# Routed experts of a four-layer transformer kernel: the gating multiply as a step of its own, the second selection and the first half's statistics one tile later

## The chip, the cores and the metric

The kernel runs on one core of one Trainium2 chip. The metric is the device time of one execution in microseconds (us), the median of several runs. The core has TensorE (PE, matrix products; its weight loads are listed as PEld), VectorE (DVE, elementwise work), ScalarE (ACT), GpSimd (POOL) and SyncE (SP, which here only issues DMAs). Each engine works through its own list of instructions in order, and waits on semaphores that other engines raise.

## The reference, cut to what matters

Four layers follow one another on 1024 tokens of 512 numbers. Each is a cross attention and a feed-forward part, each with a layer norm in front and its result added to x. The change is in the feed-forward part of the second layer, a low-rank mixture of 64 experts of rank 8, of which each token uses 16:

```python
q = einsum('bsd,rd->bsr', x, Wq_w);  scores = einsum('bsr,er->bse', q, keys)
top_vals, top_idx = top_k(scores, 16)
gate = sum(one_hot(top_idx, 64) * softmax(top_vals)[..., None], axis=-2)
z = einsum('bsd,nd->bsn', x, A_w).reshape(..., 64, 8)
z_gated = (z * gate[..., None]).reshape(..., 512)
out = einsum('bsn,on->bso', z_gated, B_w) * 2.0
x = x + out
```

Here x on the right of the first lines is the layer norm of x. What comes next, in the third layer's attention, is again a layer norm of x.

The last feed-forward part of the network (fourth layer) has weights that are to be quantised to 16 levels per block of 64 and back ("nf4") before they are used. This has nothing to do with the experts, but it is computed beside them.

## The kernel before, in words

**Tiles.** The 1024 tokens are 8 tiles of 128 (`TILES`); a half is 4 tiles (`TPH`). Everything is fp32, and a product of two fp32 matrices is done as three passes over high and low parts (helper `product`, L1739: 12 matmuls for a contraction over 512).

**The order of the work.** `schedule` writes out one list of steps for the whole program. Each engine walks the same list and, for each step, issues the instructions that its own handler of that name has. A step that stands earlier in the list stands earlier on every engine that takes part in it.

**The steps of the experts.** Per half: `route1` copies the router's scores out of PSUM and picks each token's 16 largest with two rounds of eight maxima (DVE, L1415 to L1426), ACT takes the exponentials, and `gates1` turns them into gates (DVE, L1432 to L1435). Per tile t: `z1` is the product of the normalised x with A (PE, 12 matmuls `bank<-slots,xT`); `zt1` begins on DVE with the gating multiply, `zg<-bank,gates` (L1446), which PE then transposes (4 small matmuls `bank<-ident,zg`, L1939); ACT copies the transposed tile out as the high part (`zT<-bank`, L946) and DVE takes the low part (`zT<-bank,zT`, L1201). `b1` is the product with B (PE, 12 matmuls `bank<-slots,zT`), which DVE adds to x (L1303) and, for tiles 1 to 3 of a half, follows with the statistics of the tile before (L1318). `stats` for layer index 4 ends the statistics of one half of the tokens: one more BN_STATS, 4 aggregations, a chain of 13 tiny operations with a wait behind each, and 4 normalisations into `xn` (L1224 to L1245).

In the loop over tiles PE's order is: transposes of tile t, `b1` of tile t-1, `z1` of tile t+2. So `z1` runs one tile ahead of its use and `b1` one tile behind.

**The background.** `with_background` spreads the steps of the nf4 work over the list between `q0` of the first layer and `raw_gate2` of the third, in proportion to the table `WEIGHT` of the real steps. Each block of weights takes 15 steps `nf`: DVE compares the weights with a bound (`nf_y<-nf_w`, L1681) and PE adds the result up (`nf_sum`, one matmul, L2109). The buffer `nf_y` has 6 places (`STAIR_RING`), so DVE's step i waits for PE's sum i-6. At a block's end come a wait for all its sums and `nf_w<-bank,nf_a` (L1691); the next block begins with `nf_w<-nf_w,nf_r` (L1675), and SP loads and stores each block.

**The weights.** Each chunk of weights is loaded by SP into `staging`, then split: ACT writes the high part (`slots<-staging`, L961), POOL the low part (L864). The slot of a chunk is reused after its last product; the split of the first of the `k2` weights, step `("split", 59)`, waits for `z1` of tile 7 on ACT. `spread_splits` places the splits in the list.

**Banks.** PE's products take 7 PSUM banks in turn (`claim`), and each claim waits for the last reader of what stood there.

Of the kernel before, what the change touches and what calls it, by code (L numbers as in the profile page):

```python
# [19 lines left out]
TPH = TILES // 2  # L20
# [85 lines left out]
def schedule(only=None):  # L106

    steps = []
# [61 lines left out]

    steps += [("route1", 0), ("turn", 3, 1), ("raw_route1", 1), ("z1", 0), ("gates1", 0)]
    for t in range(TILES):
        if t + 1 < TILES:
            steps.append(("z1", t + 1))
        steps.append(("zt1", t))
        if t >= 1:
            steps.append(("b1", t - 1))
        if t < 2:
            steps.append(("route1", 1) if t == 0 else ("gates1", 1))
        if t - 1 == TPH - 1:  # L180
            steps.append(("stats", 4, 0))
    steps += [("b1", TILES - 1)] + [("k2", c) for c in range(KT)] + [("bias2",), ("c2",), ("turn", 4, 0), ("stats", 4, 1)]
    if only == 4:
# [176 lines left out]
def build(nc, a, out, known, only=None):  # L360
    ctx = ExitStack()
    with ctx:
        sig = Signals(nc, ctx, known)

        def sb(name, shape, dt, scope=ctx):
            return scope.enter_context(nc.sbuf_tensor(name, shape, dt))
# [56 lines left out]
        k2 = sb("k2", [P, 2, KT, B * CTX], F32R, l)  # L423
# [59 lines left out]
        def psum(key):  # L483
            return banks[sig.bank_for(key)]
# [100 lines left out]


        base = schedule(only)
        if only is None or only == 7:
            jobs = []
# [37 lines left out]
        steps = []  # L627
# [45 lines left out]
        else:  # L673
            n_chunks = len(chunks)
            steps = [(kind, i) for i in range(n_chunks) for kind in ("load", "split")] + base
# [15 lines left out]
        def weight(name, part):  # L691

            _, p, dims, _, dest, _ = chunks[chunk_no[name]]
            if dest is not None:
                return dest[part]
            size = int(np.prod(dims))
            return flat(slots[0:p, slot_no[name] % NSLOT, part, 0:size], dims)
# [143 lines left out]
        def split_source(i):  # L841
            _, p, dims, *_ = chunks[i]
            return flat(staging[0:p, i % 2, 0:int(np.prod(dims))], dims)
# [3 lines left out]
        def _(pool):  # L847
# [12 lines left out]
            def split(i):  # L860
                pool.wait_ge(*sig.when("weight_high", i))
                _, p, dims, *_ = chunks[i]
                hi, lo = weight(chunks[i][0], 0), weight(chunks[i][0], 1)
                g.tensor_tensor(lo, split_source(i), hi.bitcast(FP32), ALU.subtract).then_inc(*sig.mark("weight_low", i))  # L864
# [323 lines left out]
        def _(dve):  # L1188
# [9 lines left out]
            def low(stage, key, dst, src, hi):  # L1198

                dve.wait_ge(*sig.when(f"{stage}_high", key))  # L1200
                v.tensor_tensor(dst, src, hi.bitcast(FP32), ALU.subtract).then_inc(*sig.mark(f"{stage}_low", key))  # L1201
# [236 lines left out]
            def z1(t):  # L1438
                pass

            def zt1(t):
                dve.wait_ge(*sig.when("z1_product", t))
                dve.wait_ge(*sig.when("gates1", t // TPH))
                if t >= 2:
                    dve.wait_ge(*sig.when("zt1_product", t - 2))
                v.tensor_tensor(zg[:, t % 2].rearrange("p (e r) -> p e r", e=NE),  # L1446
                                psum(("z1", t))[:].rearrange("p (e r) -> p e r", e=NE),
                                gates[:, t].unsqueeze(2).broadcast_to((P, NE, RANK)), ALU.mult)\
                    .then_inc(*sig.mark("gated1", t))
                low("zt1", t, zT[:, t % 2, 1], psum(("zt1", t))[:].rearrange("p (k n) -> p k n", k=KT), zT[:, t % 2, 0])  # L1450

            def b1(t):
# [231 lines left out]
            def nf_end(n, m, f):  # L1684
# [3 lines left out]
                if m == 2:  # L1688
# [3 lines left out]

            handlers = {"stats": stats, "turn": turn, "k0": k0_, "kc0": kc0_, "q0": q0_, "scores0": scores0,
                        "scale0": scale0, "low3": low3, "pv0": pv0, "o0": o0, "up0": up0, "down0": down0, "scores1": scores1,
                        "probs1": probs1, "gates1": gates1, "pv1": pv1, "router1": router1, "route1": route1, "z1": z1, "zt1": zt1, "b1": b1, "k2": k2_,
                        "m2": m2_, "bias2": bias2, "gate2": gate2, "moe": moe, "hid2": hid2, "out2": out2,
                        "values3": values3, "scores3": scores3, "pv3": pv3, "o3": o3, "up3": up3,
                        "down3": down3, "nf_max": nf_max_, "nf": nf, "nf_end": nf_end}
# [496 lines left out]
```

## Time and profile before

| | |
|---|---|
| median of 3 runs | 1546.58 us (1543.73, 1546.64, 1546.58) |
| profiled execution | 1543.49 us, span in the trace 1541.8 us |
| busy over the span | PE 1374.1 us (89%), DVE 974.8 (63%), ACT 459.4 (30%), POOL 288.6 (19%) |
| chain of waits, by engine | PE 72%, DVE 18%, issue 3%, DMA 2%, ACT 2% |
| the experts' tiles | from the first `zg` at 893.3 us to the last add to x, 972.5 us |

The profile comes from one execution, and times inside it are counted from the start of its span. The chain of waits follows the work that ended last back to its releasers. PE ends the program almost everywhere, so a gap of PE is the first thing to look for in a stage. In the rows below, "[4.67 <-DVE zg L1446]" behind a row says that the engine sat idle for 4.67 us in front of it and that the write of `zg` ended that. Rows of the timeline merge like instructions in a run: the first number is the start, the second the time from the first's start to the last's end.

### The profile page before, as it was taken

What the parts mean: (1) busy time and instruction counts of PE and PEld (TensorE: products, weight loads), DVE (VectorE), ACT (ScalarE), POOL (GpSimd) and SP (SyncE); (2) the same over time, 40 slices, a digit from 0 to 9 for tenths busy, and PEclk for the clock granted to TensorE, in tenths of its full rate; (3) what the DMA queues carried; (4) which work ended last, traced back from release to release, by engine and by line L of the source; (5) the groups of instructions that cost most, each with busy time, mean ns of one, the idle gap of its engine ahead of it and who ended that gap; (6) DMA issues with size and microseconds to landing.
All of it is one profiled execution on the core that took longest, in us unless ns stands there. A gap on an engine that the chain in (4) does not pass through costs nothing.

```text
span 1541.8 us, 18547 instructions
## 1 busy us (share of the span) xinstructions
PE 1374.1 (89%) x6429; PEld 1060.3 (69%) x6429; DVE 974.8 (63%) x2208; ACT 459.4 (30%) x991; POOL 288.6 (19%) x170
## 2 busy tenths in 40 slices
PE   6699799999999998997976687788999899899998
PEld 5467577777777666876854365656888677678886
DVE  3677767868787865554588756875447677455142
ACT  3343324332443432421324100332221453222010
POOL 4110111111111111210212001312452331022120
PEclk9889899999999999999997699999999899799999
DMA  4412423233222321222213001310111100012001
GB/s 150 143 51 61 116 78 108 74 102 92 71 80 62 112 57 57 67 65 69 88 35 76 27 28 47 102 36 2 55 55 44 53 28 1 1 41 68 26 20 55
DMA packets 99389, 96.38 MB, mean 63 GB/s; under 512 B 13122, under 2 KB 72402, under 8 KB 99298
## 3 DMA queue, kind: packets, MB, share of 16 engines
q1 hardware_dynamic: 98786, 94.35, 21.0%
q8 instruction: 54, 0.88, 0.2%
q0 software_dynamic: 512, 0.85, 0.2%
q14 instruction: 37, 0.30, 0.1%
HBM read 84.34 MB, written 10.82 MB: 62 GB/s over the span
## 4 chain that ended last, share of the span: by engine, by line
PE 72%; DVE 18%; issue 3%; DMA 2%; ACT 2%; SPq 2%; POOL 1%; DVEq 0%; ACTq 0%
PE bank L1739 51%; PE bank L2109 6%; PE bank L1833 5%; DVE nf_y L1681 3%; PE bank L1823 2%; PE bank L2044 2%; PE bank L2064 2%; PE bank L1766 1%; DVE xn L1245 1%; DVE st L1318 1%; PE bank L2053 1%; PE bank L1824 1%; DVE xT L1201 1%; DVE rs L1212 1%; DVE st L1224 1%
## 5 line engine op out<-in xcount | busy, mean ns | idle before, releaser
L1739 PE MATMUL bank<-xT,slots 128*128 128x512 f32 (+1 forms) x1920 | 459.0, 396 | 5.0 <-DVE xT L1201 3.2
L864 POOL TENSOR_TENSOR slots<-staging,slots 128x1024 fp32r<-128x1024 f32 (+4 forms) x97 | 229.4, 2367 | 1074.5 <-ACT slots L961 1074.4
L1739 PEld LDWEIGHTS bank<-xT,slots 128*128 128x128 f32 (+1 forms) x1920 | 348.1, 182 | 102.2 <-issue 9.3
L1681 DVE TENSOR_SCALAR nf_y<-nf_w 128x512 fp32r<-128x512 f32 (+2 forms) x495 | 244.8, 523 | 29.7 <-PE bank L2109 28.4
L2109 PE MATMUL bank<-nf_y,nf_d 128*128 128x512 f32 (+2 forms) x495 | 164.2, 416 | 19.7 <-DVE nf_w L1691 11.7
L1739 PE MATMUL bank<-slots,h 128*128 128x512 f32 (+1 forms) x728 | 176.5, 401 | 4.5 <-DVE h L1344 4.5
L1739 PEld LDWEIGHTS bank<-slots,h 128*128 128x128 f32 (+1 forms) x728 | 139.0, 191 | 39.3 <-DVE h L1344 5.4
L961 ACT ACTIVATE slots<-staging 128x1024 fp32r<-128x1024 f32 (+4 forms) x97 | 98.1, 1018 | 189.5 <-PE bank L1739 175.5
L2109 PEld LDWEIGHTS bank<-nf_y,nf_d 128*128 128x128 f32 (+1 forms) x495 | 92.2, 192 | 59.2 <-issue 28.8
L995 ACT ACTIVATE e<-bank,mx 128x320 f32<-128x320 f32 x128 | 66.4, 523 | 211.0 <-DVE mx L1282 207.5
L1833 PE MATMUL bank<-eT,v 128*96 128x256 f32 (+1 forms) x384 | 111.1, 412 | 0.0
L1301 DVE TENSOR_TENSOR x<-bank,x 128x512 f32<-128x512 f32 x56 | 38.7, 691 | 113.3 <-PE bank L1739 113.3
L1766 PE MATMUL bank<-ident,xn 128*128 128x128 f32 x256 | 52.4, 357 | 49.8 <-DVE xn L1245 47.0
L1739 PE MATMUL bank<-slots,q 96*128 96x512 f32 x384 | 95.5, 397 | 1.1 <-DVE q L1201 1.1
L1201 DVE TENSOR_TENSOR q<-bank,q 96x256 fp32r<-96x256 f32 (+1 forms) x96 | 48.7, 508 | 70.1 <-ACT q L946 69.7
L1739 PEld LDWEIGHTS bank<-slots,q 96*128 96x128 f32 x384 | 71.6, 188 | 18.8 <-issue 2.2
L1766 PEld LDWEIGHTS bank<-ident,xn 128*128 128x128 f32 x256 | 40.5, 181 | 61.2 <-issue 50.0
L1833 PEld LDWEIGHTS bank<-eT,v 128*96 128x96 f32 (+1 forms) x384 | 57.6, 170 | 34.7 <-issue 25.0
L1823 PE MATMUL bank<-ident,e 128*128 128x128 f32 x256 | 49.1, 287 | 31.9 <-DVE e L1289 31.7
L1739 PE MATMUL bank<-k,q 96*128 96x320 f32 x384 | 69.6, 317 | 2.8 <-DVE q L1201 2.8
L1739 PEld LDWEIGHTS bank<-k,q 96*128 96x128 f32 x384 | 62.2, 193 | 10.1 <-DVE q L1201 3.9
L1823 PEld LDWEIGHTS bank<-ident,e 128*128 128x128 f32 x256 | 34.7, 148 | 38.9 <-issue 19.9
(251 smaller groups left out, 1678.0 us busy)
## 6 DMA issues: line engine op xcount, KB each, us to landing
staging<-in_L_wqkT SPq DMA_DIRECT2D x16, 480.0 KB, 3.7
nf_out<-nf_w SPq DMA_DIRECT2D x30, 256.0 KB, 2.1
staging<-nf_out SPq DMA_DIRECT2D x30, 256.0 KB, 2.9
staging<-in_L_woT SPq DMA_DIRECT2D x16, 384.0 KB, 3.7
staging<-in_L_w SPq DMA_DIRECT2D x12, 512.0 KB, 3.7
nf_r<-nf_rcp SPq DMA_DIRECT2D x40, 128.0 KB, 3.1
nf_a<-nf_max SPq DMA_DIRECT2D x40, 128.0 KB, 3.5
xn<-in_L_w SPq DMA_DIRECT2D x20, 256.0 KB, 3.9
```

Source lines behind the costliest of these rows:

```text
L864: g.tensor_tensor(lo, split_source(i), hi.bitcast(FP32), ALU.subtract).then_inc(*sig.mark("weight_low", i))
L961: sc.activation(weight(name, 0), split_source(i), ACT.Copy).then_inc(*sig.mark("weight_high", i))
L995: sc.activation(e0[:, (2 * n + i) % E0_RING], psum(("scores0", n, i))[:, 0:KEYS0], ACT.Exp, bias=mx[:, n % 4, i:1 + i], accum_out=sm[:, n ...
L1201: v.tensor_tensor(dst, src, hi.bitcast(FP32), ALU.subtract).then_inc(*sig.mark(f"{stage}_low", key))
L1301: v.tensor_tensor(x[:, t], src, x[:, t], ALU.add).then_inc(*sig.mark(*mark))
L1681: v.tensor_scalar(nf_y[0:rows, i % STAIR_RING, 0:size], w_, bound, first, compare, ALU.mult)\
L1739: ins = mm(dst, l_, r_, start=i == 0, stop=i == len(passes) - 1)
L1766: ins = nc.tensor.transpose(bank[:, i * P:(i + 1) * P], xn[:, i, c * P:(c + 1) * P], ident[:])
L1823: nc.tensor.transpose(b0[:, (2 * k + i) * P:(2 * k + i + 1) * P], e0[:, (2 * n + i) % E0_RING, k * P:(k + 1) * P], ident[:])
L1833: ins = mm(bank[0:HD0, 0:S], v0[0:p, t, g * HD0:(g + 1) * HD0], eT0[0:p, n % 2, k], start=k == 0, stop=k == 2)
L2044: mm(bank[:], q3[:, c, t * P:(t + 1) * P], kd3[:, n % KEYS3_RING].rearrange("p h k -> p (h k)"), start=True, stop=True)\
L2109: mm(banks[NF_BANK][0:rows, 0:size], nf_d[0:rows, j - 1, 0:rows], nf_y[0:rows, i % STAIR_RING, 0:size], start=j == 1, stop=j == NPART).the ...
```

## The change

Three steps of the list move, and one is cut out of another:

- the gating multiply becomes a step `gate1` of its own, which stands in front of `z1` of the next tile and not behind it. Only DVE has a handler for it; `zt1` on DVE keeps the low part alone;
- `route1` of the second half goes from behind `zt1` of tile 0 to behind `zt1` of tile 1, and `gates1` of the second half one tile later too;
- `stats` of the first half goes from behind `b1` of tile 3 to behind `b1` of tile 4.

```diff
     for t in range(TILES):
+        steps.append(("gate1", t))
         if t + 1 < TILES:
             steps.append(("z1", t + 1))
         steps.append(("zt1", t))
+        if t == 1:
+            steps.append(("route1", 1))
         if t >= 1:
             steps.append(("b1", t - 1))
-        if t < 2:
-            steps.append(("route1", 1) if t == 0 else ("gates1", 1))
-        if t - 1 == TPH - 1:
+        if t == 2:
+            steps.append(("gates1", 1))
+        if t - 1 == TPH:
             steps.append(("stats", 4, 0))
...
-            def zt1(t):
+            def gate1(t):
                 dve.wait_ge(*sig.when("z1_product", t))
                 dve.wait_ge(*sig.when("gates1", t // TPH))
                 if t >= 2:
...
                     .then_inc(*sig.mark("gated1", t))
+
+            def zt1(t):
                 low("zt1", t, zT[:, t % 2, 1], psum(("zt1", t))[:].rearrange("p (k n) -> p k n", k=KT), zT[:, t % 2, 0])
```

`gate1` has no entry in `WEIGHT`. The background keeps its order and its place among the other steps but for a few `nf` steps, and the splits and loads stay where they were.

VectorE, tiles 0 and 1. The block from COPY to the two subtractions `r<-r,top` is `route1` of the second half; the `zg` row is the gating multiply of tile 1. Before:

```order
L1681 TENSOR_SCALAR nf_y<-nf_w 128x512
L1415 COPY r<-bank 128x256
L1419 MAX top<-r 128x8 x4
L1422 MATCH_REPLACE r<-top,r 128x64 x4
L1419 MAX top<-r 128x8 x4
L1422 MATCH_REPLACE r<-top,r 128x64 x4
L1426 TENSOR_TENSOR r<-r,top 128x256 x2
L1681 TENSOR_SCALAR nf_y<-nf_w 128x512
L1691 SCALAR_TENSOR_TENSOR nf_w<-bank,nf_a 128x4x128
L1681 TENSOR_SCALAR nf_y<-nf_w 128x512 x2
L1446 TENSOR_TENSOR zg<-bank,gates 128x512
```

VectorE at the same place in the changed program:

```order
L1686 TENSOR_SCALAR nf_y<-nf_w 128x512
L1449 TENSOR_TENSOR zg<-bank,gates 128x512
L1686 TENSOR_SCALAR nf_y<-nf_w 128x512
L1696 SCALAR_TENSOR_TENSOR nf_w<-bank,nf_a 128x4x128
L1686 TENSOR_SCALAR nf_y<-nf_w 128x512
L1204 TENSOR_TENSOR zT<-bank,zT 128x512
L1686 TENSOR_SCALAR nf_y<-nf_w 128x512
L1418 COPY r<-bank 128x256
L1422 MAX top<-r 128x8 x4
```

The gating multiply of tile 1 has moved in front of the selection and of the block's end `nf_w<-bank,nf_a`; the selection now follows the low part of tile 1.

VectorE, around the end of the first half's statistics (BN_STATS of L1224 to the normalisations `xn`). The `zg` row is tile 5. Before:

```order
L1303 SCALAR_TENSOR_TENSOR x<-bank,x 128x512
L1318 BN_STATS st<-x 128x6
L1323 COPY rt<-x 1x1
L1681 TENSOR_SCALAR nf_y<-nf_w 128x512 x2
L1224 BN_STATS st<-x 128x6
L1227 BN_AGGR mv<-st 128x2 x4
...
L1245 TENSOR_SCALAR xn<-x,mv,rs 128x512 x4
L1681 TENSOR_SCALAR nf_y<-nf_w 128x512 x2
L1446 TENSOR_TENSOR zg<-bank,gates 128x512
```

In the changed program the first `zg` row is tile 5 and the second tile 6:

```order
L1326 COPY rt<-x 1x1
L1686 TENSOR_SCALAR nf_y<-nf_w 128x512 x2
L1449 TENSOR_TENSOR zg<-bank,gates 128x512
L1686 TENSOR_SCALAR nf_y<-nf_w 128x512 x2
L1204 TENSOR_TENSOR zT<-bank,zT 128x512
L1686 TENSOR_SCALAR nf_y<-nf_w 128x512
L1306 SCALAR_TENSOR_TENSOR x<-bank,x 128x512
L1686 TENSOR_SCALAR nf_y<-nf_w 128x512 x2
L1227 BN_STATS st<-x 128x6
...
L1248 TENSOR_SCALAR xn<-x,mv,rs 128x512 x4
L1449 TENSOR_TENSOR zg<-bank,gates 128x512
```

The statistics stood in front of the gating of tile 5; they now stand in front of that of tile 6.

TensorE, tiles 0 and 1 (`ident,zg` are the transposes of a tile, `ident,rawT` those of the second half's scores). Before:

```order
L1939 MATMUL bank<-ident,zg 128x128 x4
L2109 MATMUL bank<-nf_y,nf_d 128x512
L1925 MATMUL bank<-ident,rawT 128x64 x4
L1739 MATMUL bank<-slots,xT 128x512 x12
L2109 MATMUL bank<-nf_y,nf_d 128x512 x4
L1939 MATMUL bank<-ident,zg 128x128 x4
L1739 MATMUL bank<-slots,zT 128x512 x12
```

In the changed program:

```order
L1944 MATMUL bank<-ident,zg 128x128 x4
L2114 MATMUL bank<-nf_y,nf_d 128x512
L1744 MATMUL bank<-slots,xT 128x512 x12
L2114 MATMUL bank<-nf_y,nf_d 128x512 x4
L1944 MATMUL bank<-ident,zg 128x128 x4
L1930 MATMUL bank<-ident,rawT 128x64 x4
L1744 MATMUL bank<-slots,zT 128x512 x12
```

On TensorE only the four small transposes of the scores have moved, by one tile. SyncE's and GpSimd's orders are the same in both programs, and ScalarE's differs by one exponential that goes behind one more `zT` copy.

## Rows read from the trace of the kernel before

**Rows 1.** Waits of TensorE, 886 to 973 us: us in total, times, longest.
```profile
PE bank L1939 <- DVE zg L1446: 20.3, 8, 5.0
```

**Rows 2.** Windows: stretch, length, busy us of PE, PEld, DVE, ACT, POOL, PEclk, DMA, GB/s.
```profile
893.30:972.50 79.20, 59.04 (x243) 46.17 (x244) 48.52 (x127) 8.04 (x12) 4.71 (x2) 0.91 0.15 46
903.90:909.90 6.00, 6.00 (x17) 4.88 (x18) 1.02 (x2) 0.60 (x1) 0.00 (x0) 0.53 0.29 91
```

**Rows 3.** Timeline of TensorE, tile 2 to tile 3: start us, us, what.
```profile
914.84 0.66 PE L1939 MATMUL bank<-ident,zg 128*128 128x128 f32 x4 [0.98 <-DVE zg L1446]
915.25 3.04 PE L1739 MATMUL bank<-slots,zT 128*128 128x512 f32 x12
918.13 0.62 PE L2109 MATMUL bank<-nf_y,nf_d 128*128 128x512 f32 x2
918.59 2.92 PE L1739 MATMUL bank<-slots,xT 128*128 128x512 f32 x12
921.35 0.86 PE L2109 MATMUL bank<-nf_y,nf_d 128*128 128x512 f32 x3
```

**Rows 4.** Timeline of VectorE, gating of tile 3, then tile 4.
```profile
921.78 0.76 DVE L1681 TENSOR_SCALAR nf_y<-nf_w 128x512 fp32r<-128x512 f32 x2 [1.16 <-PE bank L2109]
922.45 0.68 DVE L1446 TENSOR_TENSOR zg<-bank,gates 128x512 f32<-128x512 f32 x1
...
926.70 0.69 DVE L1303 SCALAR_TENSOR_TENSOR x<-bank,x 128x512 f32<-128x512 f32 x1 [1.43 <-PE bank L1739]
...
931.18 0.68 DVE L1446 TENSOR_TENSOR zg<-bank,gates 128x512 f32<-128x512 f32 x1
```

**Rows 5.** Timeline of TensorE, transposes of tiles 1, 5, 6 and 7.
```profile
903.88 1.11 PE L1939 MATMUL bank<-ident,zg 128*128 128x128 f32 x4 [4.67 <-DVE zg L1446]
...
944.30 1.11 PE L1939 MATMUL bank<-ident,zg 128*128 128x128 f32 x4 [4.99 <-DVE zg L1446]
...
957.00 0.81 PE L1939 MATMUL bank<-ident,zg 128*128 128x128 f32 x4 [3.81 <-DVE zg L1446]
...
965.53 0.66 PE L1939 MATMUL bank<-ident,zg 128*128 128x128 f32 x4 [2.60 <-DVE zg L1446]
```

**Rows 6.** Timeline of VectorE, 890 to 963 us.
```profile
890.09 0.42 DVE L1432 TENSOR_TENSOR r<-r 128x256 f32<-128x256 f32 x1
...
891.55 0.42 DVE L1681 TENSOR_SCALAR nf_y<-nf_w 128x512 fp32r<-128x512 f32 x1
...
897.04 0.42 DVE L1415 COPY r<-bank 128x256 f32<-128x256 f32 x1
...
901.25 0.42 DVE L1681 TENSOR_SCALAR nf_y<-nf_w 128x512 fp32r<-128x512 f32 x1
...
909.97 0.69 DVE L1303 SCALAR_TENSOR_TENSOR x<-bank,x 128x512 f32<-128x512 f32 x1 [3.29 <-PE bank L1739]
...
937.35 0.67 DVE L1224 BATCH_NORM_STATS2 st<-x 128x6 f32<-128x512 f32 x1
...
942.89 0.75 DVE L1681 TENSOR_SCALAR nf_y<-nf_w 128x512 fp32r<-128x512 f32 x2
...
949.31 0.69 DVE L1303 SCALAR_TENSOR_TENSOR x<-bank,x 128x512 f32<-128x512 f32 x1 [2.15 <-PE bank L1739]
...
953.82 2.53 DVE L1681 TENSOR_SCALAR nf_y<-nf_w 128x512 fp32r<-128x512 f32 x1
...
962.05 0.69 DVE L1303 SCALAR_TENSOR_TENSOR x<-bank,x 128x512 f32<-128x512 f32 x1 [2.83 <-PE bank L1739]
```

**Rows 7.** Timeline, first split of the `k2` weights on ScalarE.
```profile
952.59 1.06 ACT L961 ACTIVATE slots<-staging 128x1024 fp32r<-128x1024 f32 x1 [6.48 <-PE bank L1739]
```

**Rows 8.** Timeline of GpSimd: low parts of two chunks.
```profile
953.72 2.34 POOL L864 TENSOR_TENSOR slots<-staging,slots 128x1024 fp32r<-128x1024 f32 x1 [109.86 <-ACT slots L961]
...
992.88 2.34 POOL L864 TENSOR_TENSOR slots<-staging,slots 128x1024 fp32r<-128x1024 f32 x1 [0.65 <-ACT slots L961]
```

**Rows 9.** Timeline of VectorE beside the second of these.
```profile
992.87 3.99 DVE L1245 TENSOR_SCALAR xn<-x,mv,rs 128x512 f32<-128x512 f32 x4
```

More of the change, by code:

```diff
@@ L1694, in _ @@
                         "scale0": scale0, "low3": low3, "pv0": pv0, "o0": o0, "up0": up0, "down0": down0, "scores1": scores1,
-                        "probs1": probs1, "gates1": gates1, "pv1": pv1, "router1": router1, "route1": route1, "z1": z1, "zt1": zt1, "b1": b1, "k2": k2_,
+                        "probs1": probs1, "gates1": gates1, "pv1": pv1, "router1": router1, "route1": route1, "z1": z1, "gate1": gate1, "zt1": zt1, "b1": b1, "k2": k2_,
                         "m2": m2_, "bias2": bias2, "gate2": gate2, "moe": moe, "hid2": hid2, "out2": out2,
```

## The prediction

> **What bounds the stage.** I read the chain of waits first: 72% of it is TensorE, 18% VectorE, so what counts is where PE stands still. The waits of PE alone, over the stretch of the experts' tiles, show one entry [rows 1]: 20.3 us in eight waits, all for `zg`, one per tile, the longest 5.0. The windows say that PE is busy for 59.0 of the stretch's 79.2 us and DVE for 48.5, ACT and POOL far less [rows 2]: no engine is full, PE and DVE wait for each other by turns. The timeline of an ordinary tile shows why. PE does transposes, `b1`, two sums, `z1`, three sums, and then stands for 0.98 us for the next `zg` [rows 3]. On DVE this `zg` (922.45) stands behind two `nf_y` that began at 921.78, released by the first of PE's three sums (921.35) [rows 3, 4]: DVE may not write the ring of six before PE has summed, and PE sums only behind `z1`. So the gating multiply, whose inputs are long there, waits for the end of the product that it should run beside. In four places more stands in front of it [rows 5]: 4.67 us at tile 1 (the second half's selection and a block's end), 4.99 at tile 5 (the first half's statistics), 3.81 at tile 6, 2.60 at tile 7. With the two of 0.98 at tiles 2 and 3 that leaves 2.3 of the 20.3 for tiles 0 and 4.
>
> The stalls also cost clock. In the stretch after tile 1's stall the granted clock is 0.53, so nearly all of it at 1.2 GHz, and PE is busy all the time [rows 2]. From the transposes to the add to x, tile 1 takes 909.97 - 903.88 = 6.09 us and tile 6 962.05 - 957.00 = 5.05 [rows 5, 6]; at full clock it is 915.25 + 3.04 + 0.04 - 914.84 = 3.49 [rows 3] (0.04 is a typical semaphore step). Tile 5 takes 949.31 - 944.30 = 5.01, with one more sum, which at full clock is 3.72. Slow clock therefore costs 2.6 + 1.3 + 1.6 = 5.5 us.
>
> **The sizes I use.** Starts of PE [rows 3] give transposes 0.41, `b1` 2.88, a sum 0.23, `z1` 2.76: a tile without a stall is 0.41 + 2.88 + 0.46 + 2.76 + 0.69 = 7.20 us, against the 8.35 that the trace has with its stall (914.84 to 923.19, which is 922.45 + 0.68 + 0.06) [rows 3, 4]. The stall in starts is then 1.15 where the row says 0.98, since a row counts from the end of the last matmul; eight times 0.17 is 1.4, so 21.7 us of stalls in starts. On DVE an `nf_y` costs 0.33 (921.78 to 922.45 for two), `zg` 0.74 until PE has it, the second selection 901.25 - 897.04 = 4.21, `gates1` 891.55 - 890.09 = 1.46, the statistics 942.89 - 937.35 = 5.54 [rows 4, 6]. An add to x, a BN_STATS, a `zT` low part I take at 0.61, 0.60 and 0.61: the row's time less the 0.07 by which two DVE instructions overlap.
>
> **The change, tile by tile.** No instruction is added or removed; only what stands in front of what. Let T be the start of a tile's transposes. What remains as a stall is DVE's way to the next `zg` less PE's 7.20.
> - Tile 0: `zg` now stands directly behind the gates, which are done at 891.6 [rows 6], while PE still runs `z1`. No stall.
> - Tile 1: in front of `zg` stand the low part of tile 0 (begun 1.35 after T, through PE's 0.66 [rows 3] and a copy on ACT that I take at 0.6; nothing hangs on 0.3 of it), 0.61, the next block's start 0.7 and an `nf_y` 0.33: with `zg` 3.7. PE needs 0.41 + 0.23 + 2.76 + 0.92 = 4.3 for what it has. No stall; the 4.67 goes, and so does its slow clock.
> - Tile 2: here the selection comes back. Behind T of tile 1: 1.4 until the block's end and the low part's input are through, then 0.61 + 0.33 + 4.21 + 0.33 + 0.61 (add to x) + 0.67 + 0.74 = 8.9. PE needs 7.20 + 0.4 for the scores' transposes. Stall 1.3.
> - Tile 3: the add to x is ready at 3.49; then 0.61 + 0.60 + 0.67 + 1.46 (gates) + 0.74, in all 7.57. Stall 0.4.
> - Tile 4: from the add to `zg` before it was 931.18 - 926.70 = 4.48 [rows 4]; two `nf_y` of it now stand behind, so 3.81. 3.49 + 3.81 + 0.74 = 8.04. Stall 0.8.
> - Tile 5: the statistics no longer stand here: 3.49 + 0.61 + 0.60 + 0.05 + 0.67 + 0.74 = 6.2. No stall, no slow clock; the 4.99 goes.
> - Tile 6: the statistics stand here now. One sum comes first, so the add is ready at 3.72; 0.61 + 0.67 + 5.54 + 0.74 make 11.28, against 7.43 for PE. That alone would be a stall of 3.85. But a new neighbour is there. The split of the first `k2` chunk on ACT is released by `z1` of tile 7 [rows 7], 3.0 us after that product's start, and POOL follows 1.13 behind it [rows 8]. In the new order `z1` of tile 7 starts at 0.41 + 0.23 + 2.88 + 0.46 = 3.98, so POOL works from 8.1 to 10.45, and the statistics run from 5.0 to 10.54. Before, this very split met an `nf_y`, which took 2.53 instead of 0.42 [rows 6], and another one met the `xn` normalisations, which took 3.99 [rows 8, 9], where a whole statistics step with its `xn` took 5.54. So the last 2.4 us of the statistics wait until POOL is through: 2.35 more, and a stall of 6.2.
> - Tile 7: in front of its `zg` stand the same instructions as before (add, BN_STATS, an `nf_y`, the block's end, an `nf_y`). From the add to the transposes 965.53 - 962.05 = 3.48 stays [rows 5, 6], a stall of 2.8.
>
> What remains is 1.3 + 0.4 + 0.8 + 6.2 + 2.8 = 11.5 of 21.7 us. That is 10.2 us less. Of the slow clock one piece stays, behind tile 6. Its price lies between the 1.3 and the 2.6 of the three measured pieces; the 6.2 us stall is longer than any of them, so I take 2.6, and 2.9 of 5.5 are saved. Stalls of 1.3 or less cost no clock in the trace (tile 3's `b1` after 0.98). Sum: 13.1 us.
>
> The Trainium skill, page SBUF — State Buffer, section SBUF: two separate sides, has a rule that speaks against this move: DVE and GpSimd share one pair of ports, and it is an exclusive lock held for a whole instruction, so that the loser blocks fully. By it the tile-6 stall is 6.2 and the sum 13.1; if the two merely shared bandwidth, the hold would be a fraction of 2.35, and the sum near 15. The rows on the held `nf_y` and `xn` agree with the lock.
>
> **What is behind the stage.** Everything from tile 7's transposes on stands in the same order on all five engines and is started by events of this stage, so it moves forward as a block. SP starts each background block's loads from DVE events of the block before, which come earlier too. The claimed banks turn in the same rhythm, each freed at least a tile ahead.
>
> The sum against the profiled execution: 1543.49 - 13.1 = 1530.4. The median of the runs is 3.1 above that execution, and the three runs fall into 1543.7 and twice 1546.6; the changed kernel may be measured in either, 1530.4 to 1533.5. I say 1532.5.
>
> **The rivals.**
> (a) No collision at tile 6: the split comes later, or meets only DVE work that it does not hold. The stall is 3.85 and the clock piece 1.3 to 2.0: 3 to 3.5 us more, about 1529. For it: the overlap that I work out depends on 2.4 us. Against: the statistics last 5.5, and the split cannot come before `z1` of tile 7 or long after.
> (b) The clock stays at 1.2 GHz behind tile 6's long stall, since a second stall (2.8) follows after one tile's work. The last 24 expert matmuls and their sums, some 6.5 us of PE, would then take up to twice as long: 4 to 6 us less gain, 1536.5 to 1538.5. For it: 6.2 is longer than any stall before. Against: after 4.67 and 4.99 one tile's work was enough to get back to full speed.
> (c) The gain is partly given back to splits that meet the next statistics otherwise, or to a block's load that arrives late on DVE's nearer schedule: two or three holds of 2.1 to 2.35, 1537 to 1541. For it: one such hold stands at 992.87 already [rows 9]. Against: the order there does not change.
> (d) The change does not do what it says, since `nf_y` waits or a bank claim stop PE in `zg`'s place: within 2 us of before, 1545.
> (e) Slower: as (b), but the low clock lasts beyond the stage, through the `k2` and `m2` products and the start of the attention. It decides once more than 13 us of PE's full-speed work run at 1.2 GHz, since each costs its own length again; at this stage's share of PE work (59.0 of 79.2 [rows 2]) 27 us hold 20 of it, so 20 - 13 = +7: about 1552. Against it: in the trace the clock comes back within 6 us of work.
>
> **How the numbers follow.** My forecast 0.60, (a) 0.12, (b) 0.15, (c) 0.06, (d) 0.04, (e) 0.03. The forecast's own range is 1529.5 to 1535.5 (the two groups of runs, clock piece 1.3 or 3.5, each stall right to 0.5). (a) and (b) carry the range to 1527 and 1539. A change of 0.2%, 3.1 us, is about what a measurement of this kernel can tell from none: (a), (b), nearly all of (c) and the forecast are faster by more, 0.93; (d) is no change, 0.04; (e) slower, 0.03.
>
> **What would show it.** Waits of PE for `zg` sum to 10 to 11 us instead of 20.3, with four of 1.4 or less, nothing at tiles 0, 1 and 5, and one of about 6 at tile 6. The statistics of the first half last 7.9 us and contain one instruction of over 2 us beside POOL. The clock piece at tile 1 and tile 5 is gone. The stage, from the first `zg` to the last add, takes about 67.5 us instead of 79.2 (its first `zg` itself comes 1.7 earlier, without moving PE by more than 1). I am wrong if PE waits over 3 us anywhere else in the stage, or if the time after the stage is longer by more than 2 us.

## The result, and the profile after

| | before | after |
|---|---|---|
| median of 4 runs | 1545.59 us (1543.73 to 1546.64) | 1525.48 us (1524.26 to 1529.50) |
| ratio | | 0.9877, 95% interval 0.9856 to 0.9898 |
| profiled execution | 1543.49, span 1541.8 | 1524.26, span 1522.5 |
| busy | PE 1374.1 (89%), DVE 974.8 (63%) | PE 1366.3 (90%), DVE 973.9 (64%) |

The change is 20.1 us faster. I had said 1532.5, at least 1527.0: the sign is right, the time is lower than the whole range.

The waits of TensorE from 870 to 973 us (in total, times, longest), to be held against [rows 1], are 10.3 us in five, where 20.3 in eight stood:

```profile
PE bank L1944 <- DVE zg L1449: 10.3, 5, 5.7
```

The timeline of TensorE after, which answers to [rows 5], has all eight transposes of `zg` (tiles 0 to 7) here. Start, us, what, and in brackets the idle time in front:

```profile
888.21 0.60 PE L1944 MATMUL bank<-ident,zg 128*128 128x128 f32 x4
...
892.56 0.60 PE L1944 MATMUL bank<-ident,zg 128*128 128x128 f32 x4
...
901.51 0.66 PE L1944 MATMUL bank<-ident,zg 128*128 128x128 f32 x4 [1.06 <-DVE zg L1449]
...
909.07 0.66 PE L1944 MATMUL bank<-ident,zg 128*128 128x128 f32 x4 [0.19 <-DVE zg L1449]
...
917.11 0.66 PE L1944 MATMUL bank<-ident,zg 128*128 128x128 f32 x4 [0.71 <-DVE zg L1449]
...
924.33 0.60 PE L1944 MATMUL bank<-ident,zg 128*128 128x128 f32 x4
...
937.59 1.12 PE L1944 MATMUL bank<-ident,zg 128*128 128x128 f32 x4 [5.71 <-DVE zg L1449]
938.36 4.47 PE L1744 MATMUL bank<-slots,zT 128*128 128x512 f32 x12
...
946.36 0.66 PE L1944 MATMUL bank<-ident,zg 128*128 128x128 f32 x4 [2.60 <-DVE zg L1449]
```

Tiles 0, 1 and 5 have no wait, tile 6 has the long one, tile 7 keeps the 2.60 of before. `b1` behind the long wait takes 4.47 us, where [rows 3] has 3.04. VectorE beside it shows what filled that wait, the statistics, to be held against [rows 6]:

```profile
929.28 0.69 DVE L1227 BATCH_NORM_STATS2 st<-x 128x6 f32<-128x512 f32 x1
...
932.41 0.16 DVE L1213 TENSOR_TENSOR rt<-rs 128x4 f32<-128x4 f32 x1
932.60 2.19 DVE L1214 TENSOR_TENSOR rt<-rt 128x4 f32<-128x4 f32 x1
...
935.02 1.91 DVE L1248 TENSOR_SCALAR xn<-x,mv,rs 128x512 f32<-128x512 f32 x4
936.86 0.68 DVE L1449 TENSOR_TENSOR zg<-bank,gates 128x512 f32<-128x512 f32 x1
...
942.87 0.69 DVE L1306 SCALAR_TENSOR_TENSOR x<-bank,x 128x512 f32<-128x512 f32 x1 [2.75 <-PE bank L1744]
```

An operation on four numbers per partition takes 2.19 us; its like elsewhere in the same chain, the row in front of it for one, take 0.16 or 0.17. GpSimd's row, against [rows 8]:

```profile
932.42 2.35 POOL L867 TENSOR_TENSOR slots<-staging,slots 128x1024 fp32r<-128x1024 f32 x1 [91.40 <-ACT slots L964]
```

To compare executions I cut each trace in three: the **entry**, up to the start of the last operation of `gates1` of the first half; the **stage**, from there to the first product of the `k2` weights (`bank<-ctxT,slots`); and the **rest**. The windows of the stage, columns as in [rows 2], before and then after, the second row of after being the stretch behind the long wait:

```profile
891.21:972.55 81.34, 61.05 (x252) 47.45 (x251) 49.66 (x129) 8.09 (x12) 4.71 (x2) 0.92 0.15 45
```

```profile
886.42:953.38 66.96, 56.70 (x252) 44.83 (x251) 49.44 (x129) 8.09 (x12) 4.73 (x2) 0.95 0.18 55
937.50:942.90 5.40, 5.31 (x17) 4.38 (x18) 2.45 (x7) 1.54 (x2) 2.38 (x1) 0.63 0.15 51
```

The spans differ by 19.3 us. The stage gives 14.4 of it (81.34 - 66.96). The rest is 569.2 and 569.1, the same. But 4.8 lie in front of the stage (891.2 and 886.4), where the two kernels have the same instructions in the same order on every engine. That had to be explained first.

### The profile page after: what moved, and what is told of

Same layout as the page of the kernel before. It is cut to its first block, busy times and chain, and to the rows that moved or that the text cites. A ratio compares the mean times of both kernels' runs of the same rounds, so it can differ in the third digit from the quotient of the medians.

```text
span 1522.5 us, 18547 instructions
## 1 busy us (share of the span) xinstructions
PE 1366.3 (90%) x6429; PEld 1056.7 (69%) x6429; DVE 973.9 (64%) x2208; ACT 459.7 (30%) x991; POOL 288.5 (19%) x170
## 4 chain that ended last, share of the span: by engine, by line
PE 72%; DVE 18%; issue 3%; DMA 2%; ACT 2%; SPq 2%; POOL 1%; DVEq 0%; ACTq 0%
PE bank L1744 52%; PE bank L2114 6%; PE bank L1838 5%; DVE nf_y L1686 3%; PE bank L1828 2%; PE bank L2049 2%; PE bank L2069 2%; PE bank L1771 1%; DVE xn L1248 1%; DVE st L1321 1%; PE bank L2058 1%; DVE rs L1215 1%; DVE xT L1204 1%; PE bank L1829 1%; DVE x L1306 1%
## 5 line engine op out<-in xcount | busy, mean ns | idle before, releaser
L1744 PE MATMUL bank<-slots,h 128*128 128x512 f32 (+1 forms) x728 | 179.7, 407 | 4.5 <-DVE h L1347 4.5
L2114 PE MATMUL bank<-nf_y,nf_d 128*128 128x512 f32 (+2 forms) x495 | 163.0, 414 | 19.8 <-DVE nf_w L1696 11.8
L998 ACT ACTIVATE e<-bank,mx 128x320 f32<-128x320 f32 x128 | 66.4, 523 | 210.8 <-DVE mx L1285 208.1
```

What stands on the lines that cost most here:

```text
L998: sc.activation(e0[:, (2 * n + i) % E0_RING], psum(("scores0", n, i))[:, 0:KEYS0], ACT.Exp, bias=mx[:, n % 4, i:1 + i], accum_out=sm[:, n ...
L1744: ins = mm(dst, l_, r_, start=i == 0, stop=i == len(passes) - 1)
L2114: mm(banks[NF_BANK][0:rows, 0:size], nf_d[0:rows, j - 1, 0:rows], nf_y[0:rows, i % STAIR_RING, 0:size], start=j == 1, stop=j == NPART).the ...
```

## The experiments

"Half" in this table is the time in the stretch, in us, that the record of the granted clock shows at 1.2 GHz; mean is that of all runs of the kernel with its standard error. The runs come from more than one chip: the kernel before averages 1546.3 us (29 runs) on one and 1547.2 (17) on another, so that differences of 1 or 2 us between kernels are not to be relied on.

| kernel | span | entry (half) | stage (half) | rest (half) | mean (runs) | ratio to before, 95% |
|---|---|---|---|---|---|---|
| before | 1541.8 | 891.2 (112.6) | 81.3 (13.7) | 569.2 (54) | with the controls 1546.3 ± 0.6 (53) | |
| control | 1544.4 | 891.1 (109.2) | 84.5 (23.9) | 568.7 (54) | | 1.0008 [0.9984, 1.0032] |
| control2 | 1542.8 | 889.6 (105.8) | 84.5 (23.9) | 568.7 (54) | | |
| control3 | 1536.0 | 885.5 (102.4) | 84.95 (23.9) | 565.6 (47) | | |
| after | 1522.5 | 886.4 (102.4) | 67.0 (6.8) | 569.1 (54) | with its repeats 1529.8 ± 1.5 (12) | 0.9877 [0.9856, 0.9898] |
| again | 1537.5 | 897.2 (129.7) | 67.3 (6.8) | 573.0 (61) | | 0.9907 [0.9874, 0.994] |
| again2 | 1531.6 | 891.3 (116.1) | 67.4 (6.8) | 572.9 (61) | | |
| again3 | 1533.5 | 897.5 (122.9) | 66.9 (6.8) | 569.1 (54) | | |
| gate_only | 1527.3 | 887.4 (105.8) | 70.9 (10.2) | 569.1 (54) | 1533.9 ± 1.3 (6) | 0.9927 [0.9901, 0.9954] |
| gate_route | 1527.6 | 890.7 (112.6) | 67.7 (6.8) | 569.2 (54) | 1529.2 ± 0.9 (6) | 0.9897 [0.9871, 0.9924] |
| moves_only | 1538.8 | 891.6 (112.6) | 76.7 (10.2) | 570.5 (57) | 1544.7 ± 1.4 (10) | 0.9984 [0.9961, 1.0008] |
| no_hold | 1527.1 | 890.9 (112.6) | 67.3 (10.2) | 568.8 (54) | 1528.8 (1) | |
| early | 1512.7 | 886.8 (102.4) | 55.3 (0.0) | 570.6 (57) | 1518.0 ± 1.7 (6) | 0.9807 [0.9778, 0.9836] |
| early_late_stats | 1525.6 | 892.8 (116.1) | 62.8 (6.8) | 570.1 (57) | 1528.3 ± 1.0 (4) | 0.9874 [0.9844, 0.9904] |

### control and again: where the 4.8 us in front of the stage came from

No edit: the two kernels once more.

> The kernel before, unchanged, as one of the measured kernels. In the first comparison the stage itself (first gating multiply to the transposes of tile 7) gave back 14.4 us, but the changed kernel had entered the stage 4.8 us earlier although nothing before it differs. Theory A (chance): that entry time varies from execution to execution with where the granted clock falls to half. Then this run's entry (the end of the first half's gates, 891.6 us before, 886.9 changed) lies anywhere between about 885 and 894, the stage waits stay at 20.3 us, ratio within 0.3% of 1. Theory B (systematic): the entry is a property of the program. Then it is within 0.5 us of 891.6 again.

> The changed kernel once more. Both theories: waits of TensorE for the gating in the stage 10.3 us in five waits, first gating multiply to tile 7's transposes 59.4 us. Theory A: the entry is not tied to 886.9 but lies where chance puts it, and over five rounds the ratio is 0.9905 (14.4 of 1545) give or take 0.2%. Theory B: entry within 0.5 us of 886.9, ratio 0.9875.

The windows of `again`: the stage, and the first 300 us of the program, below it the same 300 us of the first execution of the changed kernel.

```profile
897.15:964.49 67.34, 57.09 (x253) 45.12 (x251) 49.43 (x129) 8.10 (x12) 4.73 (x2) 0.95 0.18 54
0.00:300.00 300.00, 258.78 (x1243) 194.05 (x1244) 193.01 (x467) 106.45 (x274) 53.35 (x32) 0.92 0.33 96
```

```profile
0.00:300.00 300.00, 259.51 (x1269) 196.14 (x1270) 196.42 (x476) 108.94 (x280) 53.41 (x32) 0.94 0.34 99
```

The same kernel enters the stage at 897.2 where it had entered at 886.4; its first 300 us have a lower granted clock (0.92 against 0.94) and hold 26 fewer matmuls, though the order up to the stage is the same. So the gain in front of the stage was chance, not the change: what varies is how long the clock stays at 1.2 GHz there (102.4 us in the one, 129.7 in the other). The stage repeats to 0.4 us. `control` brought something I had not thought of: its stage takes 84.5 us, not 81.3.

### control2, control3, again2, again3: is a stage's time a property of the kernel?

No edit. One execution with a trace each.

> The kernel before once more, for its trace. Open: over all runs so far the change is worth 17.7 us in the mean, but the two profiled executions first compared differ by 14.4 in the stage. From the first gates to the first k2 product the kernel before took 81.3 us once and 84.5 once, the changed one 67.0 and 67.3. Theory A (the kernel before loses more to slow clock in the stage than its first profiled execution showed, since each of its long waits can leave a tile at 1.2 GHz or not): this run takes 82 to 87 us, with the same 20.3 us of waits. Theory B (81.3 is the rule, 84.5 the exception, and the mean is off by chance of the entry): 81 to 82. In both the entry lies anywhere from 886 to 898.

> As control2, a further execution. Theory A: 82 to 87 us from the first gates to the first k2 product. Theory B: 81 to 82.

> The changed kernel, for its trace. Theory A: 67 to 68.5 us from the first gates to the first k2 product, since it has one long wait and so one slow piece of 1.8 to 2.6. Theory B: the same. If it takes over 70, the spread of the stage is as large in the changed kernel, and A falls.

> As again2, a further execution: 67 to 68.5 us by both theories.

The stage of the kernel before takes 81.3, 84.5, 84.5 and 84.95 us, that of the changed kernel 67.0, 67.3, 67.4 and 66.9. The time at 1.2 GHz in it is 23.9 us in all three controls, where it was 13.7, and 6.8 in all four of the changed kernel. The entries run from 885.5 to 897.5 over all the traces, with no instruction in front of the stage that differs. The stage in `control`, with the stretches behind tile 5's and tile 6's waits:

```profile
891.10:975.63 84.53, 64.22 (x252) 50.05 (x251) 49.67 (x129) 8.08 (x12) 4.70 (x2) 0.86 0.15 43
943.80:950.00 6.20, 6.16 (x17) 5.03 (x18) 1.02 (x2) 0.60 (x1) 0.00 (x0) 0.53 0.00 1
957.80:963.80 6.00, 5.92 (x17) 4.87 (x18) 0.71 (x2) 1.54 (x2) 2.36 (x1) 0.54 0.42 120
```

Its waits for `zg` are again 20.3 us in eight. What differs is the clock: 0.86 and 64.22 us of busy PE, where the execution that I had predicted from has 0.92 and 61.05. The transposes of tiles 5, 6 and 7, and the adds to x that end their products:

```profile
943.84 1.11 PE L1939 MATMUL bank<-ident,zg 128*128 128x128 f32 x4 [4.99 <-DVE zg L1446]
...
957.88 1.11 PE L1939 MATMUL bank<-ident,zg 128*128 128x128 f32 x4 [3.81 <-DVE zg L1446]
...
967.33 1.11 PE L1939 MATMUL bank<-ident,zg 128*128 128x128 f32 x4 [2.60 <-DVE zg L1446]
```

```profile
950.21 0.69 DVE L1303 SCALAR_TENSOR_TENSOR x<-bank,x 128x512 f32<-128x512 f32 x1 [3.50 <-PE bank L1739]
...
963.84 0.69 DVE L1303 SCALAR_TENSOR_TENSOR x<-bank,x 128x512 f32<-128x512 f32 x1 [3.44 <-PE bank L1739]
...
972.10 0.69 DVE L1303 SCALAR_TENSOR_TENSOR x<-bank,x 128x512 f32<-128x512 f32 x1 [1.90 <-PE bank L1739]
```

These are 6.37, 5.96 and 4.77 us, against 3.72, 3.49 and 3.49 at full clock: 2.65, 2.5 and 1.3 too long. With tile 1 (909.52 - 903.79 = 5.73, so 2.2) the slow clock costs 8.6 us; taken in the same way it is 8.6 in `control2` and 9.0 in `control3`. In the execution that I used it was 5.5, the difference being the 3.1 by which its stage is shorter. Same waits, same instructions, but there tile 5's slow piece is 1.35 shorter, tile 6's 0.9, tile 7's is absent, and tile 1's is 0.4 longer. When the stage is entered does not decide it: `control` enters 0.1 us from the first execution, `control3` 5.7 us before it, and both show 23.9.

### gate_only: the new step, without the two moves

```diff
-        if t == 1:
-            steps.append(("route1", 1))
         if t >= 1:
             steps.append(("b1", t - 1))
-        if t == 2:
-            steps.append(("gates1", 1))
-        if t - 1 == TPH:
+        if t < 2:
+            steps.append(("route1", 1) if t == 0 else ("gates1", 1))
+        if t - 1 == TPH - 1:
             steps.append(("stats", 4, 0))
```

(This and the other diffs but `moves_only`'s stand against the changed kernel.)

> Only the gating multiply as a step of its own in front of the next z1; second selection, its gates and the first half's statistics where they were. Theory 1 (each of the two long DVE blocks costs its own length wherever it stands, less what TensorE has to do): waits of 3.6 at tile 1, 0.8 at tile 4, 4.0 at tile 5, 2.8 at tile 7 (in starts), none at tiles 0, 2, 3 and 6, about 11 in all, two slow-clock pieces of 1.3 to 2.6; 12 us faster than before, so 2 to 3 us slower than the full change. Theory 2 (the gain came from moving the long blocks): 5 us faster than before.

Four waits are left, 3.12 at tile 1 (the selection), 0.70 at tile 4, 4.32 at tile 5 (the statistics) and 3.44 at tile 7:

```profile
PE bank L1942 <- DVE zg L1447: 11.6, 4, 4.3
```

By means it is 12.4 ± 1.4 us faster than before, as the first theory had it: the step `gate1` carries some three quarters of the 16.5, and the moves the remaining 4.1 ± 2.0. The 3.44 at tile 7, where 2.8 in starts was expected, has an `nf_y` of 2.60 us beside GpSimd's work in front of it, as in `gate_route` below.

### moves_only: the two moves, without the new step

```diff
             steps.append(("z1", t + 1))
         steps.append(("zt1", t))
+        if t == 1:
+            steps.append(("route1", 1))
         if t >= 1:
             steps.append(("b1", t - 1))
-        if t < 2:
-            steps.append(("route1", 1) if t == 0 else ("gates1", 1))
-        if t - 1 == TPH - 1:
+        if t == 2:
+            steps.append(("gates1", 1))
+        if t - 1 == TPH:
             steps.append(("stats", 4, 0))
```

> Only the moves: second selection, its gates and the first half's statistics one tile later, the gating multiply still behind z1 and the background steps. Theory 1 (the multiply's own place is what pays; a long block waits wherever it stands): waits for the gating 18 to 20 us in all, about 7.8 at tile 6, 2.3 at tiles 1 and 2; total 0 to 4 us faster than before. Theory 2 (the moves pay on their own): 7 us faster or more.

The eight waits stay (0.88, 2.00, 1.89, 1.20, 1.38, 0.88, 7.45, 2.60):

```profile
PE bank L1941 <- DVE zg L1448: 18.3, 8, 7.4
```

The long wait has gone from tile 5 to tile 6, which now waits 7.45 where it waited 3.81. The ratio 0.9984 [0.9961, 1.0008] is not told apart from no change; by means it is 1.6 ± 1.5 us. That the moves pay more once `zg` stands in front of `z1` (the 4.1 ± 2.0 above) is likely from the waits, but the times do not show it. The profiled stage of 76.7 is 4.6 to 8.2 us shorter than the four of before: 2.0 of it are waits, the rest slow clock (10.2 us at 1.2 GHz against 13.7 and 23.9). The means do not bear out so large a gain, and why they differ stays open.

### gate_route: the full change with the statistics at their old place, one tile earlier

```diff
-        if t - 1 == TPH:
+        if t == TPH:
             steps.append(("stats", 4, 0))
```

> The full change but with the first half's statistics at their old place (behind b1 of tile 3). Theory 1: they run clear of GpSimd's split, so tile 5 waits 4.0 instead of 0, tile 6 waits 0 instead of 5.9, the rest as in the full change (1.2, 0.4, 0.8, 2.8): about 9 us of waits, 15 to 16 us faster than before, some 2 us faster than the full change. Theory 2 (moving the statistics is worth what it takes away, 5 us): 4 to 5 us slower than the full change.

The hold did not go away. The statistics end before GpSimd's work, so the 5.71 at tile 6 becomes 4.32 at tile 5; but GpSimd's work now meets an `nf_y` of the background, and tile 7 waits 3.45 instead of 2.60. VectorE and GpSimd:

```profile
942.80 2.61 DVE L1686 TENSOR_SCALAR nf_y<-nf_w 128x512 fp32r<-128x512 f32 x1
```

```profile
942.71 4.93 POOL L867 TENSOR_TENSOR slots<-staging,slots 128x1024 fp32r<-128x1024 f32 x2 [99.32 <-ACT slots L964]
```

I had expected 2 us from it; by means it is 0.6 ± 1.7 faster than the full change, no difference.

### no_hold: the split behind tile 6's `zg`

```diff
+        if known and ("split", 59) in steps:
+            steps.remove(("split", 59))
+            steps.remove(("load", 61))
+            at = steps.index(("zt1", 6))
+            steps[at + 1:at + 1] = [("split", 59), ("load", 61)]
```

> The full change, with the split of the first k2 chunk (and the load behind it) one place later, behind the transposes of tile 6, so that GpSimd does not work beside the first half's statistics. Theory 1 (the lock costs 2.0 of tile 6's 5.7 us wait): tile 6 waits 3.7, and from the transposes of tile 5 to those of tile 6 it is 11.3 us instead of 13.3; the two splits now follow one another on GpSimd and hold a comparison later, so tile 7 waits 3.5 to 5 instead of 2.6, and the stage gains little. Theory 2 (the statistics are long for a reason of their own): tile 6 waits 5.7 as before.

TensorE, transposes of tiles 5, 6 and 7 with the products behind the last two:

```profile
928.84 0.60 PE L1950 MATMUL bank<-ident,zg 128*128 128x128 f32 x4
...
940.08 1.12 PE L1950 MATMUL bank<-ident,zg 128*128 128x128 f32 x4 [3.68 <-DVE zg L1455]
940.85 5.40 PE L1750 MATMUL bank<-slots,zT 128*128 128x512 f32 x12
...
949.79 1.12 PE L1950 MATMUL bank<-ident,zg 128*128 128x128 f32 x4 [2.63 <-DVE zg L1455]
950.56 6.91 PE L1750 MATMUL bank<-slots,zT 128*128 128x512 f32 x24
```

No instruction of the statistics is held, and tile 6's wait is 3.68, in starts 3.85, which is what the prediction had worked out without a hold. From tile 5 to tile 6 it is 11.24 us instead of 13.26 (937.59 - 924.33): the hold costs 2.0 us. Yet the stage is 67.3, no shorter, because the slow clock lasts longer: 10.2 us at 1.2 GHz instead of 6.8, `b1` of tile 6 5.40 instead of 4.47, and tile 7's product slow as well, which is 2.3 us more than in the first execution of the full change. This is one execution; whether the longer slow stretch belongs to the shorter wait or is chance it cannot say. I had expected tile 7's wait to grow to 3.5 or more; it did not.

### early and early_late_stats: `zg` one tile ahead

```diff
+    steps.append(("gate1", 0))
     for t in range(TILES):
-        steps.append(("gate1", t))
         if t + 1 < TILES:
             steps.append(("z1", t + 1))
         steps.append(("zt1", t))
+        if t + 1 < TILES:
+            steps.append(("gate1", t + 1))
...
-        if t - 1 == TPH:
+        if t == TPH:
             steps.append(("stats", 4, 0))
```

The gating of tile t+1 stands behind the low part of tile t, so in front of `b1`'s add to x, of the selection and of the statistics. `early_late_stats` is the same with the last edit left out.

> The gating multiply one place earlier still: that of tile t+1 directly behind the low part of tile t, in front of the add of tile t-1; selection and its gates as in the change, statistics at their old place. DVE then has 4.6 us in hand per tile. Theory 1 (waits come only from what stands on DVE between the add and the next multiply): no wait over 0.5 us for the gating in the stage, no slow clock; from the end of the first gates to the first k2 product 54 to 57 us instead of 67; 24 to 27 us faster than before. Theory 2 (DVE, busy 45 us of the stage, becomes the bound, and PE waits for the background's nf_y or the low part instead): 61 us or more for the same stretch, 16 to 20 us faster than before.

> As the kernel with the multiply earlier still, but with the statistics behind b1 of tile 4 as in the change, so that they meet GpSimd's split. Theory 1: they hold DVE for 7.6 us, 1 to 3 us more than it has in hand, so one wait of 1 to 3 us at tile 7, and the stretch is 1 to 3 us longer than with the statistics at the old place. Theory 2 (the meeting with the split does not matter once there is slack): the same within 0.5 us.

The window of `early`'s stage, then its one wait for `zg`, at tile 7:

```profile
886.79:942.13 55.34, 54.56 (x253) 43.57 (x251) 48.78 (x129) 8.10 (x12) 5.26 (x2) 1.00 0.21 61
```

```profile
934.76 0.65 PE L1946 MATMUL bank<-ident,zg 128*128 128x128 f32 x4 [0.67 <-DVE zg L1451]
```

TensorE is busy for 54.56 of 55.34 us, at full clock throughout. GpSimd still holds an `nf_y` (2.52 us at 930.99), but VectorE is far enough ahead for it not to matter. `early` takes a mean of 1518.0 us and beats both kernels: 28.3 below before, 11.8 below the change (standard error of this last one 2.2). The stage of 55.3 is what the first theory had; its one wait is a little over the 0.5 allowed, the gain a little over the 24 to 27.

`early_late_stats` was to lose 1 to 3 us against that; its stage is 7.4 longer, and its mean 10.4 ± 2.0. On VectorE two instructions in a row are held by two splits in a row (GpSimd works from 936.43 to 941.18), and TensorE stops for the background's sums, whose `nf_y` stand behind the statistics:

```profile
936.62 2.27 DVE L1216 TENSOR_TENSOR rt<-rt 128x4 f32<-128x4 f32 x1
938.92 2.28 DVE L1217 SCALAR_TENSOR_TENSOR rs<-rt,rs 128x4 f32<-128x4 f32 x1
```

```profile
943.54 0.84 PE L2116 MATMUL bank<-nf_y,nf_d 128*128 128x512 f32 x2 [3.95 <-DVE nf_y L1688]
...
946.13 1.12 PE L1946 MATMUL bank<-ident,zg 128*128 128x128 f32 x4 [1.76 <-DVE zg L1451]
```

The wait at tile 7 is as forecast. But both theories had looked at `zg` alone. Making one hand-off early left the other, `nf_y` to PE's sum, behind the same statistics.

## Why the prediction was wrong

**The step that failed is the slow clock**, "Slow clock therefore costs 2.6 + 1.3 + 1.6 = 5.5 us", of which 2.9 were to be saved, and with it the 13.1 of the sum. I took it from one execution. In the three other executions of the same kernel with a trace the stage is 3.2 to 3.6 us longer, and the pieces add up to 8.6, 8.6 and 9.0 us. What stays after the change is 942.87 - 937.59 = 5.28 less 3.49, 1.8 (2.2, 2.2 and 1.8 in the repeats), where I had taken 2.6. So the clock usually gives 6.8 and not 2.9. In the first two executions alone it gave 5.5 - 1.8 = 3.7. With the waits, in starts 21.66 before and 11.12 after, the usual gain is 10.5 + 6.8 = 17.3, and 84.67 - 67.14 = 17.5 is the difference of the usual stages. Over all four traces of each it is 83.84 - 67.14 = 16.7, and over all runs 1546.3 - 1529.8 = 16.5 ± 1.6.

**The second thing left out is chance, and of this miss it is the larger part.** Runs of one kernel scatter with a standard deviation of 4 to 5 us (1537.7 to 1553.1 for the one, 1523.9 to 1539.2 for the other). I had three runs that lay within 3 us of each other, and took that for the whole scatter ("the changed kernel may be measured in either"). The profiled execution of after reads: 1530.4 as predicted from the execution before, less 1.3 for a stage that gave 14.4 instead of 13.1, less 4.8 for the entry, is 1524.3; measured 1524.26. The forecast lay 7.0 us above the measured median. Had I worked with 16.7 and the mean of before, I would have said 1529.6, so 2.9 of the 7.0 can be laid to the sum, nearly all of it to the clock term. The other 4.1 are the luck of the first four runs: they average 1526.2, the eight later ones 1531.6 ± 1.8, which is inside the stated range and 0.9 from the forecast. A range for a median of four would have had to reach some 5 us to either side.

This scatter is itself the clock's. In 49 runs of the kernel before, those at a granted clock of 0.934 average 1552.7 us (4 runs), those at 0.938 1547.7 (10), those at 0.942 1542.5 (11). The four traces of each kernel show how little a few of them say of a whole time: their stages differ by 16.7 us and their spans by 10.0, since the entries and the rests came out longer in the changed kernel's four.

Point by point:

- **Waits**: right. Predicted in starts 1.3, 0.4, 0.8, 6.2 and 2.8 (11.5) at tiles 2, 3, 4, 6 and 7; the rows say 1.06, 0.19, 0.71, 5.71 and 2.60, with 0.17 each 11.1. Nothing at tiles 0, 1 and 5.
- **The hold at tile 6**: right, and shown by `no_hold` to cost 2.0 us (taken: 2.35). The statistics last 936.86 - 929.28 = 7.6 us (predicted 7.9), and one instruction takes 2.19. The Trainium skill, page SBUF — State Buffer, section SBUF: two separate sides, describes the port shared by DVE and GpSimd as an exclusive lock for a whole instruction. The trace agrees: the held operation starts at 932.60 and ends at 934.79, GpSimd's at 934.77, where a shared bandwidth would have stretched it by less. `gate_route`'s 2.61 and `early_late_stats`' 2.27 and 2.28 say the same.
- **What is behind the stage moves as a block**: right in the first pair, 569.2 and 569.1. Over the other executions it takes 565.6 to 573.0 and goes with the time at 1.2 GHz in it: 565.6 with 47 us, 568.7 to 569.2 with 54, 570.1 to 570.6 with 57, 572.9 and 573.0 with 61. Both of the last are of the changed kernel, longer by more than the 2 us that the prediction gave as a sign of being wrong. The means of four, 568.1 and 571.0, differ by 2.9 ± 1.4, and whether the change has a part in that stays open.
- **The stage**: from the first `zg` (886.95) to the end of the last add to x (953.34) it takes 66.4 us, where about 67.5 was said; no slow clock at tiles 1 and 5, one slow piece behind tile 6.
- **Rivals**: (a) is refuted by the 2.19, (b) and (e) by `b1`'s add 1.8 and not 5 late, by tile 7's product, which runs at full clock in all four executions (3.49 us from its transposes to its add), and by the unchanged rest; (c) and (d) did not happen. None of them, nor the forecast, had the case that occurred: the mechanism as told, with a term of it undersized by the sample.

What stays open: what makes the same stalls cost 5.5 us of clock in one execution and 8.6 in another, and what decides how long the clock stays at 1.2 GHz in front of the stage, by which the entry wanders by 12 us.

## What to carry to other kernels

Where engines hand work to each other through lists that are kept in order, put the step that another engine waits for directly behind its inputs, one product ahead if buffers allow; long steps that nobody waits for (a selection, statistics) come after that: moved alone, they carried the wait from one tile to the next, and the gain could not be told from none (1.6 ± 1.5 us). Look at every hand-off that stands behind such a long step, the background's included, and not only at the one that the wait names. And take a term that depends on the clock from several executions: here one trace had it a third too small, while waits repeated to 0.1 us.

## What the runs showed of the hardware

- **One program, several clocks.** Over the traces, all with the same instructions in front of the stage, the time at 1.2 GHz in the entry goes from 102.4 to 129.7 us. The three executions with 102.4 enter at 885.5 to 886.8, the one with 129.7 at 897.2 and one with 122.9 at 897.5. A line through all fourteen gives some 0.4 us of entry for each us at 1.2 GHz and misses none by more than 2 us.
- **The same stall, another price.** Behind tile 6's wait of 3.81 us the work took 5.05 us in one execution and 5.96 in another; behind tile 7's of 2.60 once 3.5 and once 4.77.
- **Tiny operations are held as long as big ones.** 128x4 operations of 0.16 us took 2.19, 2.27 and 2.28 beside a GpSimd instruction of 2.35, and two GpSimd instructions in a row held two operations in a row. An operation of VectorE that takes one tile from PSUM and one from SBUF was not held: in the trace before, `k<-bank,bk,k` at 978.08 took 0.48 us while GpSimd worked from 977.41 to 980.07, and the `nf_y` behind it, at 978.49, took 1.87 instead of 0.42.
